# Routed experts in tiles of 128 rows from four experts, two tiles taken together

## The reference

```
scores = softmax(norm(x) @ gate.T);  the best 6 of 64 experts, out of the best 3 of 8 groups
slot = expert * 96 + min(position, 95);  buf[slot] = norm(x)[token]      # 64 experts x 96 rows
g = buf[e] @ Wg[e].T;  u = buf[e] @ Wu[e].T                              # 96 x 176 each
out[e] = (silu(g) * u) @ Wd[e].T                                         # 96 x 256
y[token] = sum over its 6 slots of weight * out[slot];  plus a shared expert
```

## Time and profile before

| | |
|---|---|
| median of the runs | 1821.0 us (1817.26 to 1830.79, 3 runs) |
| the profiled execution | 1814.0 us, span 1812.3 us |
| mean granted TensorE clock | 0.909 of 2.4 GHz |
| busy | TensorE 1487.1 us (82%), VectorE 1089.0 (60%), ACT 732.3 (40%), POOL 775.6 (43%) |
| routed-expert stage, pass 0 and 1 | 125.4 to 300.8 us, 794.5 to 960.2 us |
| bytes moved by DMA | 145.49 MB |

### The profile page before, as it was taken

How to read it: one execution, slowest core, us unless ns; L and a number is a source line. 1 busy time by engine, 2 the same in 40 slices (tenths; PEclk the granted TensorE clock), 3 DMA queues, 4 the chain that set the end, 5 groups by cost and what they waited for, 6 DMA issues and landing times. The chain is left out here.

```text
span 1812.3 us, 39345 instructions
## 1 busy us (share of the span) xinstructions
PE 1487.1 (82%) x14334; PEld 1022.4 (56%) x14334; DVE 1089.0 (60%) x2639; ACT 732.3 (40%) x1754; POOL 775.6 (43%) x741
## 2 busy tenths in 40 slices
PE   6888995758898978889993778778898887888798
PEld 3555563425555544555662656456576665666576
DVE  6852222476776547832224888576777676664788
ACT  5533332355555425533332111355545545443211
POOL 4453333753300004543336553286766766764000
PEclk9999998679999988899996888888999999989899
DMA  8319995321100005239972221000000000000000
GB/s 248 92 46 262 283 282 170 107 67 53 36 1 1 1 22 161 59 121 279 293 217 85 77 75 52 12 2 3 14 3 2 14 3 3 14 3 3 9 17 21
DMA packets 92662, 145.49 MB, mean 80 GB/s; under 512 B 25032, under 2 KB 52528, under 8 KB 92512
## 3 DMA queue, kind: packets, MB, share of 16 engines
q1 hardware_dynamic: 62816, 93.06, 17.8%
q0 software_dynamic: 15360, 37.77, 6.9%
q10 hardware_dynamic: 14336, 12.59, 2.5%
HBM read 122.39 MB, written 18.87 MB: 78 GB/s over the span
## 5 line engine op out<-in xcount | busy, mean ns | idle before, releaser
L2323 POOL TENSOR_TENSOR sb_m_prob<-sb_m_prob,sb_m_rinv 128x512 f32<-128x512 f32 x256 | 261.4, 1043 | 144.2 <-DVE sb_m_rinv L2377 141.8
L2258 ACT ACTIVATE sb_m_prob<-m_ps_s,sb_m_nmax 128x512 f32<-128x512 f32 x256 | 173.8, 684 | 231.8 <-DVE sb_m_nmax L2381 231.8
L1264 POOL DMA_INDIRECT sb_c_rows<-slot_rows,sb_slot x192 | 192.3, 1001 | 109.1 <-issue 52.0
L2159 PE MATMUL m_ps_v<-sb_m_pT,sb_m_lat_rows 32*64 32x128 f32 x8192 | 161.4, 301 | 61.5 <-ACT sb_m_q_whole L2251 36.2
L2381 DVE TENSOR_REDUCE sb_m_nmax<-m_ps_s 128x2 f32<-128x1024 f32 x128 | 155.8, 1217 | 90.4 <-PE m_ps_s L2142 89.6
L1098 POOL DMA_INDIRECT e_xn<-xn_rows,sb_table x128 | 118.3, 925 | 208.6 <-PE e_ps_x L1176 196.2
L1247 DVE TENSOR_TENSOR sb_e_h<-sb_e_sg,e_ps_gu 96x176 f32<-96x176 f32 x128 | 42.6, 333 | 255.6 <-ACT sb_e_sg L1223 255.6
L2159 PEld LDWEIGHTS m_ps_v<-sb_m_pT,sb_m_lat_rows 32*64 32x64 f32 x8192 | 140.7, 146 | 92.2 <-issue 82.2
L1185 PE MATMUL e_ps_gu<-e_wgu,sb_e_xT 128*96 128x352 f32 x512 | 176.4, 467 | 19.8 <-ACT sb_e_xT L1217 19.2
L2388 DVE STREAM_TRANSPOSE sb_m_pT<-sb_m_prob 128x1024 f32<-128x1024 f32 x128 | 158.0, 1234 | 1.0 <-POOL sb_m_prob L2323 1.0
L2141 PE MATMUL m_ps_s<-sb_m_latT_high,sb_m_qa 128*128 128x512 f32 x256 | 130.7, 511 | 16.5 <-ACT sb_m_prob L2258 13.7
(11 more groups left out here) (278 smaller groups left out, 3103.0 us busy)
## 6 DMA issues: line engine op xcount, KB each, us to landing
e_wgu<-wgu SPq DMA_DIRECT2D x128, 352.0 KB, 4.8
e_wdn<-wdn SPq DMA_DIRECT2D x128, 192.0 KB, 4.6
slot_rows<-sb_e_y ACTq DMA_DIRECT2D x128, 96.0 KB
xn_rows<-e_xn SPq DMA_DIRECT2D x16, 256.0 KB, 2.2
sb_c_rows<-slot_rows,sb_slot POOLq DMA_INDIRECT x192, 2.8
sb_x<-x SPq DMA_DIRECT2D x4, 512.0 KB, 5.6
e_xn<-xn_rows,sb_table POOLq DMA_INDIRECT x128, 5.0
sb_g_zm<-wqT SPq DMA_DIRECT2D x1, 2048.0 KB, 8.8
```

What stands on the lines that cost most here:

```text
L1264: pool.indirect_dma_start(rows[u][j][:, :], None, k.slot_rows[:, :], bass.IndirectOffsetOnAxis(ap=k.slot[:, n, j:j + 1], axis=0))\
L2159: ins = pe.matmul(ps_v[rows_of(hh), a, 0:P], lat_rows[b % 2][rows, kb // TB, kb % TB, :], of[rows, hh, :, kb, :], start=(kb == 0), stop=(k ...
L2258: act.activation(prob[s % 4][:, hh, :], ps_s[s % 2][:, hh, :], ACT.Exp, bias=nmax[s % 2][:, hh:hh + 1], accum_out=rsum[s % 2][:, hh:hh + 1 ...
L2323: pool.tensor_tensor(part, part, rinv[s % 2][:, hh:hh + 1].to_broadcast([P, T]), ALU.mult)\
```

## The change

Four experts form a quad; 16 quads. A tile has 128 rows: rows 32t to 32t+31 of each of the four experts of a quad, so a quad has three tiles (t = 0, 1, 2), and a pass 48. TensorE transposes a tile's tokens at once (128 rows). Gate-up and down are then done per expert: the 32 columns of an expert are stationary, its weights move, and the result goes to 32 PSUM partitions of its own. Tiles are taken in pairs p, in straight code without a loop; in step p TensorE transposes the tokens of pair p and the hidden rows of pair p-2, does gate-up of pair p-1 and then down of pair p-2. Weights have 3 buffers of four experts (before: 12 of one), loaded by two larger DMAs per quad; gathered tokens have 8 buffers (before 4), down results 4 (before 2). The table is rearranged to 128 rows by 48 tiles, which takes 12 copies. A down result's 128 rows go to four places in `slot_rows`, whose layout is unchanged.

The diff, cut to its core:

```diff
-AHEAD = 12
 XB = 4
+GE = 4
+ROWS = P // GE
+THIRDS = CAP // ROWS
+QUADS = E0 // GE
+ROW_TILES = QUADS * THIRDS
+QB = 3
...
+            def load_quad(a):
+                sp.dma_start(k.wgu[a][:, :, :, :], k.w["wgu0"][a]).then_inc(k.sem(f"e_wgu_got{a}"), 16)
+                sp.dma_start(k.wdn[a][:, :, :, :], k.w["wdn0"][a]).then_inc(k.sem(f"e_wdn_got{a}"), 16)
...
             store(3)
-            load_experts(0, AHEAD // 2)
+            load_quad(0)
             store(4)
             store(5)
-            load_experts(AHEAD // 2, AHEAD)
+            load_quad(1)
             store(6)
             store(7)
+            load_quad(2)
...
-            pool.wait_ge(table_ready, r + 1)
-            for e in range(XB):
-                gather_expert(pool, k, e, k.gathered[e])
+            for t in range(XB):
+                if t < THIRDS:
+                    pool.wait_ge(table_ready, r * THIRDS * GE + (t + 1) * GE)
+                gather_rows(pool, k, t)
...
-            dve.tensor_copy(k.table[:, :], kept_table).then_inc(table_ready, 1)
+            for t in range(THIRDS):
+                for j in range(GE):
+                    dve.tensor_copy(k.table[j * ROWS:(j + 1) * ROWS, :].rearrange("p (a t) -> p t a", t=THIRDS)[:, t, :],
+                                    kept_table[t * ROWS:(t + 1) * ROWS, :].rearrange("p (a j) -> p j a", j=GE)[:, j, :])\
+                       .then_inc(table_ready, 1)
...
+            for a in range(QB, QUADS):
+                q, left = a % QB, base + (a - QB + 1) * THIRDS
+                sp.wait_ge(gu_ready, left)
+                sp.dma_start(wgu[q][:, :, :, :], k.w["wgu0"][a]).then_inc(gu_got[q], 16)
+                sp.wait_ge(dn_ready, left)
+                sp.dma_start(wdn[q][:, :, :, :], k.w["wdn0"][a]).then_inc(dn_got[q], 16)
...
+            def gate_up(t):
...
+                for c in range(DC):
+                    for j in range(GE):
+                        ins = pe.matmul(ps_gu[v][own(j), :], xT[v][:, c, own(j)], wgu[a % QB][:, j, c, :],
                                         start=(c == 0), stop=(c == DC - 1))
+                ins.then_inc(gu_ready, 1)
...
+            for p in range(PH + 2):
+                for t in both(p):
+                    tokens_turned(t)
+                for t in both(p - 2):
+                    hidden_turned(t)
+                for t in both(p - 1):
+                    gate_up(t)
+                for t in both(p - 2):
+                    down(t)
...
-                    act.dma_start(k.slot_rows.rearrange("(e c) d -> e c d", c=CAP)[s - 3], y[v][:, :])\
-                       .then_inc(y_stored[v], 16)
...
+            rows = k.slot_rows.rearrange("(a j t i) d -> a t j i d", j=GE, t=THIRDS, i=ROWS)
...
+            def stored(t):
+                v, b, g = t % 2, t % YB, base + t
+                act.wait_ge(dn_ready, g + 1)
+                if g >= YB:
+                    act.wait_ge(y_stored[b], 16 * (g // YB))
+                act.activation(y[b][:, :], ps_y[v][:, :], ACT.Copy).then_inc(y_ready, 1)
+                act.wait_ge(y_ready, g + 1)
+                act.dma_start(rows[t // THIRDS, t % THIRDS], y[b][:, :]).then_inc(y_stored[b], 16)
+
+            for p in range(PH + 2):
+                for v in range(2):
+                    for t in both(p - 1)[v:v + 1]:
+                        silu(t)
+                    for t in both(p)[v:v + 1]:
+                        tokens_copied(t)
+                for t in both(p - 2):
+                    stored(t)
...
-        "wgu0": c(gu.reshape(E0, DC, P, 2 * M0).transpose(0, 2, 1, 3)),
-        "wdn0": c(down_chunks),
+        "wgu0": c(gu.reshape(QUADS, GE, DC, P, 2 * M0).transpose(0, 3, 1, 2, 4)),
+        "wdn0": c(down_chunks.reshape(QUADS, GE, MH, 2, D).transpose(0, 2, 1, 3, 4)),
```

More of the change, by code:

```diff
@@ L1079, in _, with gather_rows @@
             k.dve_steps = s.n
[L1082 to L1095, removed]
+def gather_rows(pool, k, t):
+    u = t % (2 * XB)
     pool.sem_inc(k.sem("passed"), 1)
-    pool.indirect_dma_start(x, None, k.xn_rows[:, :], bass.IndirectOffsetOnAxis(ap=k.table[:, e:e + 1], axis=0))\
-        .then_inc(k.sem(f"e_tokens_got{e % XB}"), 16)
+    pool.indirect_dma_start(k.xn[u // 2][:, u % 2, :], None, k.xn_rows[:, :],
+                            bass.IndirectOffsetOnAxis(ap=k.table[:, t:t + 1], axis=0))\
+        .then_inc(k.sem(f"e_tokens_got{u}"), 16)
 def routed_experts(nc, k, r):
-    U, GA, LAG = AHEAD, 4, 3
-    got = [k.sem(f"e_tokens_got{u}") for u in range(GA)]
-    w_got = [k.sem(f"e_weights_got{u}") for u in range(U)]
+    U, YB = 2 * XB, 4
+    PH = ROW_TILES // 2
+    got = [k.sem(f"e_tokens_got{u}") for u in range(U)]
+    gu_got = [k.sem(f"e_wgu_got{q}") for q in range(QB)]
+    dn_got = [k.sem(f"e_wdn_got{q}") for q in range(QB)]
     xT_raw, xT_ready = k.sem("e_xT_psum_ready"), k.sem("e_xT_ready")
@@ L1113, in routed_experts @@
     dn_ready, y_ready = k.sem("e_down_ready"), k.sem("e_y_ready")
-    y_stored = [k.sem(f"e_y_stored{u}") for u in range(2)]
+    y_stored = [k.sem(f"e_y_stored{u}") for u in range(YB)]
+    base = r * ROW_TILES
     with ExitStack() as ctx:
         sb, ps = scoped(nc, ctx)
-        x = k.gathered
-        xT = [sb(f"e{r}_xT{u}", [P, DC, CAP]) for u in range(2)]
+        xT = [sb(f"e{r}_xT{u}", [P, DC, P]) for u in range(2)]
         wgu, wdn = k.wgu, k.wdn
[L1120 to L1127, removed]
-        block = ctx.enter_context(nc.Block())
[L1129 to L1141, removed]
@@ new lines, in routed_experts @@
+        sg = [sb(f"e{r}_sg{u}", [P, M0]) for u in range(2)]
+        h = [sb(f"e{r}_h{u}", [P, M0]) for u in range(2)]
+        hT = [sb(f"e{r}_hT{u}", [MH, 2, P]) for u in range(2)]
+        y = [sb(f"e{r}_y{u}", [P, D]) for u in range(YB)]
+        ps_x = [ps(f"e{r}_ps_x{u}", [P, DC, P]) for u in range(2)]
+        ps_gu = [ps(f"e{r}_ps_gu{u}", [P, 2 * M0]) for u in range(2)]
+        ps_h = [ps(f"e{r}_ps_h{u}", [MH, 2, P]) for u in range(2)]
+        ps_y = [ps(f"e{r}_ps_y{u}", [P, D]) for u in range(2)]
@@ L1143, in _, with both, quads_before, own @@
+        block = ctx.enter_context(nc.Block())
+        def both(p):
+            return [2 * p, 2 * p + 1] if 0 <= p < PH else []
+        def quads_before(q):
+            return r * len(range(q, QUADS, QB))
+        def own(j):
+            return slice(j * ROWS, (j + 1) * ROWS)
         @block.sync
         def _(sp):
[L1145 to L1150, removed]
@@ L1206, in _, with tokens_turned @@
-            pipelined(pe, step, U, last, U)
+            def tokens_turned(t):
+                u, v, g = t % U, t % 2, base + t
+                x = k.xn[u // 2][:, u % 2, :]
+                pe.wait_ge(got[u], 16 * (r * (ROW_TILES // U) + t // U + 1))
+                if g >= 2:
+                    pe.wait_ge(xT_ready, g - 1)
+                for c in range(DC):
+                    ins = pe.transpose(ps_x[v][:, c, :], x[:, c * P:(c + 1) * P], k.ident[:, :])
+                ins.then_inc(xT_raw, 1)
@@ new lines, in hidden_turned, with down @@
+            def hidden_turned(t):
+                v, g = t % 2, base + t
+                pe.wait_ge(h_ready, g + 1)
+                if g >= 2:
+                    pe.wait_ge(hT_ready, g - 1)
+                for c in range(2):
+                    ins = pe.transpose(ps_h[v][:, c, :], h[v][:, MHC[c]:MHC[c] + MH], k.ident[:, :])
+                ins.then_inc(hT_raw, 1)
+            def down(t):
+                a, v, g = t // THIRDS, t % 2, base + t
+                pe.wait_ge(hT_ready, g + 1)
+                if t % THIRDS == 0:
+                    pe.wait_ge(dn_got[a % QB], 16 * (quads_before(a % QB) + a // QB + 1))
+                if g >= 2:
+                    pe.wait_ge(y_ready, g - 1)
+                for c in range(2):
+                    for j in range(GE):
+                        ins = pe.matmul(ps_y[v][own(j), :], hT[v][:, c, own(j)], wdn[a % QB][:, j, c, :],
+                                        start=(c == 0), stop=(c == 1))
+                ins.then_inc(dn_ready, 1)
@@ L1234, in _, with tokens_copied @@
-            pipelined(act, step, U, last, U)
-            for v in range(2):
-                act.wait_ge(y_stored[v], 16 * ((r + 1) * E0 // 2))
+            rows = k.slot_rows.rearrange("(a j t i) d -> a t j i d", j=GE, t=THIRDS, i=ROWS)
+            def tokens_copied(t):
+                v, g = t % 2, base + t
+                act.wait_ge(xT_raw, g + 1)
+                if g >= 2:
+                    act.wait_ge(gu_ready, g - 1)
+                act.activation(xT[v][:, :, :], ps_x[v][:, :, :], ACT.Copy).then_inc(xT_ready, 1)
@@ new lines, in silu @@
+            def silu(t):
+                v, g = t % 2, base + t
+                act.wait_ge(gu_ready, g + 1)
+                if g >= 2:
+                    act.wait_ge(h_ready, g - 1)
+                act.activation(sg[v][:, :], ps_gu[v][:, 0:M0], ACT.Silu).then_inc(act_ready, 1)
+            def stored(t):
[6 more added lines that the diff above has]
```

(6 more changed lines are left out.)

114 lines of the change are left out of this document (27 added, 87 removed).

## The result

The changed kernel takes 1880.7 us (median of 4 runs, 1874.1 to 1893.7) against 1825.9 us before (1817.3 to 1831.4, 4 runs): ratio 1.030, interval 1.025 to 1.034. It is slower by 55 us. The profiled execution has 1880.7 us, a span of 1879.0.

A forecast was written before the change was run, and what follows sets the result against it. Routed stages were taken as bound by TensorE and DMA in turn, DMA acting through the output store. Per pass 200 + 6 + 1 = 207 us, 414 for both, +73 on 1814.0: 1887, median 1894; forecast 1890, range 1850 to 1925, lower end widened to 1800.

The forecast's parts named there:

- Four engines for the store: Output store to four blocks of 32 rows: carried by 4 DMA engines instead of 16, 12,672 packets; chance 0.75.
- TensorE's tile, 2.60 us: Routed stages: four experts' products run side by side, 2.60 us a tile, x48 = 125 us a pass against 152.
- The term of the busiest engine, 200 us of 207 a pass: Routed stages: each store-carrying engine moves 3.77 MB a pass, taken as 200 us between 187 and 217.
- the stores are no faster when quiet: Output stores: their rate when alone, 16.9 GB/s an engine, used for the lower bound and the choice of 200 us.
- My bounds of +43 and +103: Both routed stages: range around the forecast loss of +73 us.
- The start of a stage, 6 us: Routed stage's start: a buffer is free only after three tiles, so the first reload starts about 6 us in.
- What ACT does about it: ACT in the routed stages: its waits for stores to land rise well over 91 us.
- Weights at nothing ("same bytes"): Weight loads: 3 buffers of four experts, same bytes; issues fall from 104 to 26 a pass, nothing gained.
- The clock, left to the upper half: TensorE in the stages: lowered clock after gaps, up to 10.4 us a pair against DMA's 8.6; left to the range.
- The elsewhere of the sum, 0: Outside the routed stages: no change counted; only the stages' +73 us was added to the profiled 1814.0 us.
- Table: Table rearrangement on VectorE: 12 copies instead of one, 2.6 us, hidden in VectorE's idle time.
- Rival A: Output store keeps 16 engines: stages 159 + 153 us, a gain of 29, 1785 profiled, 1792 median; chance 0.18.

The follow-up runs named there:

- e1: Changed kernel with a tile's 128 result rows stored to 128 neighbouring DRAM rows instead of four blocks (values differ): 1800.9 us, ratio 0.989.
- e5: Changed kernel with tiles taking every third position of each expert, so the store has one stride over 128 rows; whole computation kept: 1803.2 us, ratio 0.988.
- e7: e5 with each weight reload bringing only two of a quad's four experts: 1771.8 us, ratio 0.969.
- e3: Changed kernel with each quad's two weight loads cut into four each, store left on four engines: 1845.9 us, ratio 1.014.
- e4: Kernel before with a result's 96 rows stored to four separate blocks of 24 rows (values differ): 1883.1 us, ratio 1.034.
- e10: Changed kernel with the stores issued from SP's queue, among the weight loads, instead of from ACT: 1858.5 us, ratio 1.020.
- e12: Changed kernel with each weight reload bringing only two of a quad's four experts: 1776.1 us, ratio 0.975.
- e8: Kernel before run once more, unchanged, for a second profile: 1825.4 us, ratio 1.001.
- e11: Kernel before with four buffers for the down result y instead of two, nothing else: 1801.9 us, ratio 0.988.

## Why the prediction was right, and where not

Forecast 1890 from four engines, measured 1880.7, inside the forecast's own range of 1850 to 1925. The cause was right; but its terms are further off than the total, and that two of them nearly cancel is luck.

- **Four engines for the store**: right. 12,672 packets, a share of 25.4% when the stores are alone, and undone in e1 and e5.
- **TensorE's tile, 2.60 us**: right. A pair takes 5.25, gate-up in four streams 1.29 a tile (2.57 for two), and e7 shows the stage at 138.
- **The term of the busiest engine, 200 us of 207 a pass**: mis-sized. The stages took 190.9 and 191.9, +42 for two passes where I had +73. My bounds of +43 and +103 were added wrongly: 187 + 7 and 217 + 7 a pass, less 341, are +47 and +107, so the stages lie 5 us under the lower one. The step that failed is "the stores are no faster when quiet" at 16.9 GB/s: 216:221 shows 0.45 MB in 5 us on four engines, 22.5 GB/s each. The rest goes at 309/16 = 19.3 GB/s (window below). From the first reload on an engine has 2.09 MB of loads and gathers, 108 us, and 1.57 MB of stores, 70 us: 178, where the trace has 316.6 - 141.9 = 174.7. But that fit proves little: e3 moves the same bytes on the same four engines in 301.4 - 140.6 = 160.8 us. So no fixed rate of an engine sets the stage; some 14 us a pass come with the large loads and ACT's holds, for which the sum had no term.
- **The start of a stage, 6 us**: too small. The first reload comes 141.91 - 125.67 = 16.2 us into the stage; 5.88 of it is one silu that waits for a remote releaser. Every version with the stage written out has such waits of 2.3 to 8.0 us there; the versions with the loop have none.
- **What ACT does about it**: half right. I had its waits for landings rise well over 91 us; they fell to 35.9, and 116.5 us stand in the store instruction instead. They rose as forecast only in e4, e3 and e10 (124.0, 127.9 and 190.1). That an instruction that only posts a transfer can hold its engine was not in my list of waits.
- **Weights at nothing ("same bytes")**: wrong beside four-engine stores. The large loads cost 35 us there (e3); with half of the bytes four engines cost next to nothing (e12).
- **The clock, left to the upper half**: it is there, 0.85 in the stages against 0.97 in e12, TensorE busy 145 us instead of 130. The fall follows the holds; how much of the 15 us lengthens the stage, no run separates.
- **The elsewhere of the sum, 0**: 21 us in the first profile's missing stall. By luck it made up for most of the 31 us by which the stages were forecast too long. Against e8 (span 1823.4) the stages account for 44.5 of 55.6 us.
- **Table**: right. 12 copies take 2.42 us (2.6 forecast), hidden: the stage starts at 125.7 us, before at 125.4.
- **Rival A**: its 159 + 153 for 16 engines is what e5 has, 158.7 + 154.2; its 1792 was 11 under the median, and its 1785 for a profiled execution 25 under that of e5, mostly for want of the same stall. That loads then hold up the new tiles, e7 bears out. Wrong was the reading that the same bytes bound the kernel before, and with it part of the first paragraph: the 84% to 97% of the DMA engines were not its bound. In 200:250 they moved 278 GB/s; in e11 they move 319 in the same window.

DMA in 205:214 of the changed kernel, and in 200:250 of e11:

```profile
205.00:214.00 9.00, 3.80 (x60) 1.69 (x52) 0.14 (x1) 0.31 (x2) 1.59 (x2) 0.90 1.01 309
```

```profile
DMA packets 8806, 15.97 MB, mean 319 GB/s; under 512 B 1360, under 2 KB 3376, under 8 KB 8806
```

Timelines of the changed kernel around the stage's start (ACT, SP) and at the table copies (VectorE; the earlier trace rows).

```profile
137.09 0.32 ACT L1229 ACTIVATE sb_e_sg<-e_ps_gu 128x176 f32<-128x176 f32 x1 [5.88 <-remote]
...
141.91 0.33 SPq L1145 DMA_DIRECT2D e_wgu<-wgu  x1
...
116.57 2.42 DVE L1083 CAST sb_table<-r_ps_t 32x16 uint32<-32x16 f32 x12 [0.67 <-PE r_ps_t L752]
```

## What to carry to other kernels

Look at a store's destination as DMA sees it: if its outermost dimension has few steps, few engines carry it (here 4 steps, four engines; 128, 96 or 32 steps, 16); another assignment of rows to positions can give the same computation one long stride. A high busy share of the DMA engines is no proof that bytes bound a stage: where an engine waits for its last store to land, give it more buffers first and see (here 22 us for two buffers of 1 KB a partition). And take a second profile of the kernel before ahead of a sum that sets one profile against a median.

## What the runs showed of the hardware

- A store instruction on ACT's queue takes 0.33 us with 16 engines (144 packets), 0.53 with four (132 packets), and 8.4 to 11.3 us when 364 to 393 packets of the queue are outstanding on four engines. On 16 engines (e5) 416 outstanding packets held nothing. So it fits a bound by packets per engine, 91 to 98 here against 26. In e3 359 were outstanding once without a hold, but nine of its store instructions took 1.0 to 1.5 us at 270 to 357. Where exactly the bound lies, no run shows.
- On the shared engines the store queue gets 2.8 packets a microsecond and engine beside loads in 11 and 8 KB rows (88 in 8 us), 22.6 without them. With rows of 2.8 and 2 KB the holds nearly vanish (e3). SP's queue had 222 packets in those 8 us, 1.7 an engine and microsecond, of some eight to eleven times the bytes. Both fit engines that share their time between the queues by packets and not by bytes, so that large packets starve the queue of small ones, though not one for one (2.8 against 1.7); that wasn't tried by itself. The Trainium skill, page "DMA: Bandwidth & Descriptors", section "Queues, rings and completion order", says of an engine that it goes round the queues that have work, a packet of one, then of the next. Its packet is a group, typically of 9 to 17 descriptors, where a packet of this profile is one row; so the trace goes with the rule in kind, and shows no such groups.
- There are waits for a remote releaser on ACT, VectorE and GpSimd, 1 to 20.5 us each; at the weight folding they are 17 to 27 us in sum in twelve profiles, and there are none in e1 and in the first of before. In the changed kernel no packet of the two instruction queues is on its way during the 18.5 us. What they wait for stays open.
